# One transformer block on one core: steps without engine loops, another order of VectorE's step, a projection in four passes

## What is computed

```python
h = ln(x)
Q, K, V = h @ wq.T, h @ wk.T, h @ wv.T              # 64 wide each
energy  = einsum('bnd,bne->bde', K, V)              # one 64x64 matrix a batch
x = x + ((Q @ energy) * sqrt(3 / 64)) @ wo.T
h = square(relu(ln(x) @ W_fc.T))                    # 1024 wide
y = h @ W_proj.T
# five steps of a leaky integrate-and-fire neuron driven by y; mean of its spikes
x = x + spikes(y) / 5
```

## Time and profile before

| what | value |
|---|---|
| median of three runs | 505.34 us |
| the profiled execution: its own time | 501.43 us |
| its span (first to last instruction) | 499.5 us |
| mean granted TensorE clock | 0.993 of full |
| TensorE busy | 478.6 us, 96% |
| VectorE busy | 342.4 us, 69% |
| ScalarE busy | 286.4 us, 57% |
| GpSimd busy | 237.3 us, 48% |
| HBM traffic | 17.7 MB read, 8.4 MB written, 52 GB/s |

### The profile page before, as it was taken

How to read it: one execution, slowest core, us unless ns; L and a number is a source line. 1 busy time by engine, 2 the same in 40 slices (tenths; PEclk the granted TensorE clock), 3 DMA queues, 4 the chain that set the end, 5 groups by cost and what they waited for, 6 DMA issues and landing times.

```text
span 499.5 us, 9518 instructions
## 1 busy us (share of the span) xinstructions
PE 478.6 (96%) x3080; PEld 432.7 (87%) x3080; DVE 342.4 (69%) x966; ACT 286.4 (57%) x519; POOL 237.3 (48%) x196
## 2 busy tenths in 40 slices
PE   7899899999999979999999997999999999999995
PEld 6698689899889869898898996898898999999995
DVE  4457658777676776767677855768867674939447
ACT  3427666657566655666566564665746664656540
POOL 1444664473736526374544634545363743535340
PEclk9999999999999999999999998999999999999998
DMA  8413021130403113040312212131110101010102
GB/s 310 99 44 69 17 42 44 54 75 36 93 0 85 43 55 73 0 126 0 85 42 64 63 43 42 43 79 47 55 30 0 42 2 42 1 43 1 44 1 84
DMA packets 60705, 26.46 MB, mean 53 GB/s; under 512 B 55552, under 2 KB 56192, under 8 KB 60416
## 3 DMA queue, kind: packets, MB, share of 16 engines
q1 hardware_dynamic: 60672, 26.09, 19.1%
HBM read 17.69 MB, written 8.39 MB: 52 GB/s over the span
## 4 chain that ended last, share of the span: by engine, by line
PE 79%; DVE 10%; issue 6%; ACT 2%; DMA 1%; POOL 1%; SPq 0%; DVEq 0%; POOLq 0%
PE hid_ps L814 10%; PE hid_ps L815 10%; PE hid_ps L816 10%; PE y_ps L816 10%; PE y_ps L815 10%; PE y_ps L814 10%; PE work_ps L856 3%; PE y_ps L823 2%; DVE stat L592 2%; PE work_ps L922 2%; DVE cnt L701 2%; PE work_ps L923 2%; DVE cnt L720 1%; PE kv_ps L814 1%; PE kv_ps L815 1%
## 5 line engine op out<-in xcount | busy, mean ns | idle before, releaser
L355 POOL TENSOR_TENSOR hid_l<-hid,hid_h 128x512 fp32r<-128x512 f32 x128 | 165.2, 1296 | 204.7 <-ACT hid_h L409 204.5
L398 ACT ACTIVATE relu<-hid_ps 128x512 f32<-128x512 f32 x128 | 76.6, 598 | 112.1 <-PE hid_ps L816 110.6
L815 PE MATMUL y_ps<-wdn_l,hid_h 128*128 128x256 f32 x480 | 136.1, 284 | 0.0
L816 PE MATMUL y_ps<-wdn_h,hid_l 128*128 128x256 f32 x480 | 136.1, 283 | 0.0
L814 PE MATMUL y_ps<-wdn_h,hid_h 128*128 128x256 f32 x480 | 135.7, 283 | 0.0
L814 PE MATMUL hid_ps<-x2T_h,wup_h 128*128 128x512 f32 x256 | 105.5, 412 | 0.5 <-ACT relu L398 0.3
L815 PE MATMUL hid_ps<-x2T_l,wup_h 128*128 128x512 f32 x256 | 100.9, 394 | 0.0
L816 PE MATMUL hid_ps<-x2T_h,wup_l 128*128 128x512 f32 x256 | 100.3, 392 | 0.0
L814 PEld LDWEIGHTS y_ps<-wdn_h,hid_h 128*128 128x128 f32 x480 | 92.0, 192 | 5.1
L815 PEld LDWEIGHTS y_ps<-wdn_l,hid_h 128*128 128x128 f32 x480 | 92.0, 192 | 4.9
L816 PEld LDWEIGHTS y_ps<-wdn_h,hid_l 128*128 128x128 f32 x480 | 91.9, 192 | 0.0
(11 more groups left out here) (125 smaller groups left out, 611.7 us busy)
## 6 DMA issues: line engine op xcount, KB each, us to landing
xs<-x_dram SPq DMA_DIRECT2D x15, 512.0 KB, 3.3
out_dram<-x SPq DMA_DIRECT2D x15, 512.0 KB, 2.7
x_block<-x_dram SPq DMA_DIRECT2D x104, 64.0 KB, 2.5
hid<-w_up_dram SPq DMA_DIRECT2D x1, 1024.0 KB, 8.1
x<-w_down_dram SPq DMA_DIRECT2D x1, 1024.0 KB, 10.2
xs<-x_dram SPq DMA_DIRECT2D x2, 256.0 KB, 2.8
out_dram<-x SPq DMA_DIRECT2D x1, 256.0 KB, 2.0
out_dram<-x SPq DMA_DIRECT2D x2, 128.0 KB, 1.9
```

Of the source, the lines that this page charges most:

```text
L355: nc.gpsimd.tensor_tensor(hid_l[:, i % 2, c, :], hid[:, c % 4, :], hid_h[:, i % 2, c, :].bitcast(f32), ALU.subtract).then_inc(hid_ready, 1)
L398: nc.scalar.activation(relu[:, c % 2, :], hid_ps[c % 2][:, :], ACT.Relu).then_inc(relu_done, 1)
L815: mm(dst, a[0], b[1], start=False, stop=False)
L816: return mm(dst, a[1], b[0], start=False, stop=stop)
```

## The change

- `steps` and SyncE's loop become plain loops of the program that writes the kernel: all 17 steps are written out, with constant semaphore counts.
- VectorE's step begins with the first six of the 12 operations that count the second pair of group i-2 (before: of group i-1, at the end of the step before). Then come `turn_blocks`, `q_low_half`, in odd steps `energy_sum`, the other six counts, in odd steps `eo_low_half`, and then `first_moments`, which stood behind `turn_blocks`. From the residual on the order is as before. GpSimd computes the inverse deviation of group i+3 at c = 4, before at c = 1.
- q takes four passes for six: the two halves of wq lie side by side in `wq_hl`, so one pass of `xT_h` gives high-weight q on partitions 0 to 63 and low-weight q on 64 to 127. Two passes of `xT_l` by the high half of wq alone (64 columns of weights) add to partitions 0 to 63. ScalarE copies only 64 partitions. VectorE takes two dependent operations for the low half: the rest of partitions 0 to 63, written across to 64 to 127 of `kv_scaled`, and then the sum with the lower half of the bank.
- The lead-in has 3, 2, 2 and 12 rounds of idle transposes where it had 8, 4, 2 and 16; ScalarE splits the up weights earlier, VectorE has group 1's `xT_low_half` ahead of its statistics, and `q_low_half(0, 0)` behind K and V of group 1.

```diff
         def steps(eng, step):
-            for i in range(0, FIRST):
-                step(0, i)
-            with eng.Fori(0, LOOPS) as r:
-                for j in range(UNROLL):
-                    step(r, FIRST + j)
-            for i in range(LAST, GROUPS + 1):
+            for i in range(GROUPS + 1):
                 step(0, i)
...
-                    if c == 1 and there(r, i + 3):
+                    if c == (1 if is_first(r, i) else 4) and there(r, i + 3):
                         inverse_deviation(r, 2 if is_first(r, i) else i + 3, 0)
...
-                nc.scalar.activation(qT[:, n % 2, :], q_bank(r, n)[:, :], ACT.Copy).then_inc(q_high, 1)
+                nc.scalar.activation(qT[0:HEAD, n % 2, :], q_bank(r, n)[0:HEAD, :], ACT.Copy).then_inc(q_high, 1)
...
             xT_high_half(0, 1)
+            half_of_columns(w_loaded["up"], wup_raw, wup_h, wup_high, 0)
             kvT_out(0, 0)
+            q_high_half(0, 0)
+            half_of_columns(w_loaded["up"], wup_raw, wup_h, wup_high, 1)
+            kvT_out(0, 1)
             kv_high_half(0, 0)
-            half_of_columns(w_loaded["up"], wup_raw, wup_h, wup_high, 0)
-            q_high_half(0, 0)
-            kvT_out(0, 1)
+            q_high_half(0, 1)
             kv_high_half(0, 1)
-            half_of_columns(w_loaded["up"], wup_raw, wup_h, wup_high, 1)
+            half_of_columns(w_loaded["down"], wdn_raw, wdn_h, wdn_high, 0)
             energy_first_half(0, PER_BATCH - 1)
-            q_high_half(0, 1)
+            half_of_columns(w_loaded["down"], wdn_raw, wdn_h, wdn_high, 1)
             eo_high_half(0, PER_BATCH - 1)
...
                 dve.wait_ge(q_high, upto(r, n + 1))
-                nc.vector.tensor_tensor(qT[HEAD:P, n % 2, :], q_bank(r, n)[HEAD:P, :],
-                                        as_f32(qT[HEAD:P, n % 2, :]), ALU.subtract).then_inc(q_ready, 1)
+                dve.wait_ge(kv_ready, 2 if isinstance(r, int) and n < 3 else upto(r, n + 1))
+                if there(r, n - 1):
+                    dve.wait_ge(q_ready, upto(r, n))
+                nc.vector.tensor_tensor(kv_scaled[HEAD:P, :], q_bank(r, n)[0:HEAD, :],
+                                        as_f32(qT[0:HEAD, n % 2, :]), ALU.subtract).then_inc(q_rest, 1)
+                dve.wait_ge(q_rest, upto(r, n + 1))
+                nc.vector.tensor_tensor(qT[HEAD:P, n % 2, :], q_bank(r, n)[HEAD:P, :], kv_scaled[HEAD:P, :], ALU.add)\
+                    .then_inc(q_ready, 1)
...
+                if there(r, i - 2):
+                    spikes(r, i - 2, 1, range(0, PAIR_OPS // 2))
                 if there(r, i + 3):
                     turn_blocks(r, i + 3)
-                    first_moments(r, i + 3)
                 if there(r, i + 2):
                     q_low_half(r, i + 2)
                 if there(r, i + 2) and closes_batch(i + 2):
                     energy_sum(r, i + 2)
+                if there(r, i - 2):
+                    spikes(r, i - 2, 1, range(PAIR_OPS // 2, PAIR_OPS))
                 if there(r, i + 2) and closes_batch(i + 2):
                     eo_low_half(r, i + 2)
+                if there(r, i + 3):
+                    first_moments(r, i + 3)
...
-                if there(r, i - 1):
-                    spikes(r, i - 1, 1, range(PAIR_OPS))
...
-                for k in range(EC):
-                    last = three(q_bank(r, n)[:, :], (wqq_h[:, k, :], wqq_l[:, k, :]),
-                                 (xT_h[:, n % 2, k, :], xT_l[:, n % 2, k, :]), k == 0, k == EC - 1)
+                both = [wq_hl[:, k, :, :].rearrange("p s d -> p (s d)") for k in range(EC)]
+                mm(q_bank(r, n)[:, :], both[0], xT_h[:, n % 2, 0, :], start=True, stop=False)
+                for k in range(EC):
+                    mm(q_bank(r, n)[0:HEAD, :], wq_hl[:, k, 0, :], xT_l[:, n % 2, k, :], start=False, stop=False)
+                last = mm(q_bank(r, n)[:, :], both[1], xT_h[:, n % 2, 1, :], start=False, stop=True)
...
-            keep_warm(8)
+            keep_warm(3)
...
-            keep_warm(4)
+            keep_warm(2)
...
-            keep_warm(16)
+            keep_warm(12)
```

More of the change, by code:

```diff
@@ L91, in build @@
         wkv_h, wkv_l = (sb(f"wkv_{s}", [P, EC, 2 * HEAD], f32r) for s in "hl")
-        wqq_h, wqq_l = (sb(f"wqq_{s}", [P, EC, 2 * HEAD], f32r) for s in "hl")
+        wq_hl = sb("wq_hl", [P, EC, 2, HEAD], f32r)
         wup_h, wup_l = (sb(f"wup_{s}", [P, EC, HID], f32r) for s in "hl")
@@ L174, in build @@
         averager_ready, mean_done = sem("averager_ready"), sem("mean_done")
-        wkv_centred, wqq_centred = sem("wkv_centred"), sem("wqq_centred")
+        wkv_centred, wq_centred = sem("wkv_centred"), sem("wq_centred")
         wkv_high, wkv_ready = sem("wkv_high"), sem("wkv_ready")
-        wqq_high, wqq_ready = sem("wqq_high"), sem("wqq_ready")
+        wq_high, wq_ready = sem("wq_high"), sem("wq_ready")
         wup_high, wup_ready = sem("wup_high"), sem("wup_ready")
@@ L188, in build @@
         kv_turned, kv_in_scale, kv_high, kv_ready = sem("kv_turned"), sem("kv_in_scale"), sem("kv_high"), sem("kv_ready")
-        q_done, q_high, q_ready = sem("q_done"), sem("q_high"), sem("q_ready")
+        q_done, q_high, q_rest, q_ready = sem("q_done"), sem("q_high"), sem("q_rest"), sem("q_ready")
         energy_done, energy_out, energy_ready = sem("energy_done"), sem("energy_out"), sem("energy_ready")
@@ L301, in _ @@
             load_blocks(0, 3)
[L303 to L309, removed]
+            for i in range(-1, GROUPS):
                 step(0, i)
@@ L519, in _ @@
             high_half_of_weights(wkv_centred, wkv_raw[:, :], wkv_h, wkv_high)
-            high_half_of_weights(wqq_centred, wqq_raw[:, :], wqq_h, wqq_high)
+            act.wait_ge(wq_centred, 1)
+            nc.scalar.activation(wq_hl[:, :, 0, :], wqq_raw.rearrange("p (k s n) -> p k s n", k=EC, s=2)[:, :, 0, :], ACT.Copy).then_inc(wq_high, 1)
             xT_high_half(0, 0)
             xT_high_half(0, 1)
+            half_of_columns(w_loaded["up"], wup_raw, wup_h, wup_high, 0)
             kvT_out(0, 0)
+            q_high_half(0, 0)
+            half_of_columns(w_loaded["up"], wup_raw, wup_h, wup_high, 1)
+            kvT_out(0, 1)
             kv_high_half(0, 0)
-            half_of_columns(w_loaded["up"], wup_raw, wup_h, wup_high, 0)
-            q_high_half(0, 0)
-            kvT_out(0, 1)
+            q_high_half(0, 1)
             kv_high_half(0, 1)
-            half_of_columns(w_loaded["up"], wup_raw, wup_h, wup_high, 1)
+            half_of_columns(w_loaded["down"], wdn_raw, wdn_h, wdn_high, 0)
             energy_first_half(0, PER_BATCH - 1)
-            q_high_half(0, 1)
+            half_of_columns(w_loaded["down"], wdn_raw, wdn_h, wdn_high, 1)
             eo_high_half(0, PER_BATCH - 1)
-            half_of_columns(w_loaded["down"], wdn_raw, wdn_h, wdn_high, 0)
-            half_of_columns(w_loaded["down"], wdn_raw, wdn_h, wdn_high, 1)
             x2T_high_half(0, 0)
@@ L564, in kv_scale @@
                     dve.wait_ge(kv_ready, upto(r, n))
+                if not isinstance(r, int) or n >= 2:
+                    dve.wait_ge(q_ready, 3 if isinstance(r, int) and n == 2 else upto(r, n))
                 by_token = rstd1[:, n % RING, :].unsqueeze(2).broadcast_to([P, TILES, 2 * HEAD])
@@ L780, in step @@
                     kv_low_half(r, i + 3)
-                if there(r, i - 1):
-                    spikes(r, i - 1, 1, range(PAIR_OPS))
             centre_weights(w_loaded["kv"], wkv_raw[:, :], 0, wkv_centred)
-            centre_weights(w_loaded["qq"], wqq_raw[:, :], 1, wqq_centred)
+            centre_weights(w_loaded["qq"], wqq_raw[:, :], 1, wq_centred)
             first_moments(0, 0)
@@ L789, in _ @@
             xT_low_half(0, 0)
-            low_half_of_weights(wqq_high, wqq_raw[:, :], wqq_h, wqq_l, wqq_ready)
+            dve.wait_ge(wq_high, 1)
+            nc.vector.tensor_tensor(wq_hl[:, :, 1, :], wqq_raw.rearrange("p (k s n) -> p k s n", k=EC, s=2)[:, :, 0, :], as_f32(wq_hl[:, :, 0, :]),
+                                    ALU.subtract).then_inc(wq_ready, 1)
+            xT_low_half(0, 1)
             first_moments(0, 1)
-            xT_low_half(0, 1)
             kv_scale(0, 0)
             kv_low_half(0, 0)
-            q_low_half(0, 0)
             kv_scale(0, 1)
             kv_low_half(0, 1)
+            q_low_half(0, 0)
             energy_sum(0, PER_BATCH - 1)
@@ L884, in project_q @@
                     pe.wait_ge(xT_ready, n + 1)
-                    pe.wait_ge(wqq_ready, 1)
+                    pe.wait_ge(wq_ready, 1)
                 else:
                     pe.wait_ge(x2T_ready, upto(r, n - 1))
+                both = [wq_hl[:, k, :, :].rearrange("p s d -> p (s d)") for k in range(EC)]
+                mm(q_bank(r, n)[:, :], both[0], xT_h[:, n % 2, 0, :], start=True, stop=False)
                 for k in range(EC):
-                    last = three(q_bank(r, n)[:, :], (wqq_h[:, k, :], wqq_l[:, k, :]),
```

(3 more changed lines are left out.)

3 lines of the change are left out of this document (removed).

## The result

The changed kernel takes 483.65 us in the median of four runs (483.2 to 484.51); the kernel before, run beside it, 504.99 (504.41 to 507.06). The ratio is 0.957, with a 95% interval of 0.954 to 0.960: faster by 4.3%. Forecast were 485 us and a range of 481 to 493. The profiled execution took 483.47 us, its span is 481.7; before it was 501.43 and 499.5.

What follows compares the result with a forecast made beforehand. TensorE's work and its waits for VectorE were taken as the bound. Terms -3.5, +0.6, -0.9, -5.5 and -9.9 sum to -19.2 us, giving a median of 486.1; 1 us allowed for clock falls made it 485, range 481 to 493.

Steps and rivals of the forecast that it cites:

- Passes of q: TensorE, every group: four passes instead of six save 0.46 us, 5.5 us over 12 groups.
- The waits: TensorE waiting for VectorE's energy in steps that close a batch: removing this saves 9.9 us.
- VectorE's schedule: Times from S, the start of TensorE's step: VectorE's energy is ready 2.1 us early, the residual has 0.7 us cover.
- Instruction loads: Steps written out instead of looped: fetching the extra instructions was priced at nothing.
- Step 0: First step: x2n's turn 0.6 us later through q's second VectorE operation; the next step 0.9 us shorter.
- The lead-in: Before the first step: fewer idle transposes and new orders save 3.5 us, bounds 2.5 to 3.8.
- The walk: Estimated schedule of the new orders before the first step, using durations from profile rows; gave the 3.5 us saving.
- rival 2: TensorE's clock falls before or in the first step, one to three times at 1.5 us: 487 to 490 us; 8%.
- VectorE late (1): In closing steps VectorE's energy or residual overruns its margin, returning 3.9 to 9 us: 489 to 494 us; 16%.
- rival 5: Waits go, but clock and the part before the first step give more than allowed: 479 to 481.5 us; 5%.
- Slow passes (3): TensorE's q passes with 64 weight columns take 0.86 us, not 0.232, giving back 17.6 us: 503 us; 3%.
- instruction loads (4): Written-out steps bring 12 more instruction packets, each stalling TensorE 2.5 us, adding 30 us: 516 us; 3%.

Runs made afterwards that it cites:

- straight_q4: Kernel before with all 17 steps written out and q in four passes, VectorE's step and lead-in in the old order: 497.76 us.
- straight_order: Kernel before with all steps written out and VectorE's step in the new order, q still in six passes, old lead-in: 491.88 us.
- new_pool: Changed kernel with GpSimd waiting for K and V of group 1 before it splits the up weights: 482.02 us.
- changed_again: Changed kernel, unaltered, timed once more in a later set: 483.94 us.
- straight_order_q4: Changed kernel with the old lead-in, except that q_low_half(0, 0) stays behind K and V of group 1: 484.44 us.
- new_warm: Changed kernel with 3 and 4 rounds of idle transposes added in two lead-in gaps where TensorE waits for K and V low halves: 483.04 us.
- new_pool_again: Changed kernel with GpSimd's weight splits behind K and V of group 1, timed again in a later set: 482.14 us.

## Why the prediction was right, and where it was not

**The windows** were right to 0.01 us. Passes of q: 0.46 us a group was forecast, 28.02 - 27.56 was measured. The pass with 64 weight columns costs 0.23, the value taken. The waits: 9.9 us were forecast; together with q's 5.5, 15.4 us between the turns at 84.22 and 455.90. Measured is 371.68 before and 356.25 after (81.71 to 437.96), 15.4.

**VectorE's schedule** was right point by point: energy ready at S+7.9 (7.85), TensorE there at S+10.0 (9.9), residual at S+14.3 with 0.7 of cover (14.3 and 0.59). `straight_q4` and `straight_order` show that this order is what makes the passes pay. The prediction's sum added the two terms without saying that the passes' 5.5 us hold only with the new order: under the old one they cost 1.6.

**Instruction loads** at nothing were right: 23 packets, no idle TensorE. The 2.5 us at a branch back was shown twice, by taking it away and by putting it back (2.10 us).

**Step 0** was forecast 0.6 later and the step behind it 0.9 shorter. From the first matmul of step 0 to the turn that waits for x2n it was 18.76 and is 19.22, +0.5; from there to the next turn 27.84 and 26.80, -1.0.

**The lead-in** was the term that was wrong in size: -3.5 us, with 2.5 to 3.8 as its bounds, and the first matmul of step 0 moved from 37.62 to 35.85, -1.8; x2n's first turn, a sign named for about 31 us, began at 32.53. The part up to K and V was right. Their first matmuls, before and after:

```profile
13.11 0.48 PE L814 MATMUL kv_ps<-xT_h,wkv_h 128*128 128x512 f32 x1
```

```profile
11.11 0.50 PE L815 MATMUL kv_ps<-xT_h,wkv_h 128*128 128x512 f32 x1
```

The walk had 11.05. From there to step 0 it had 23.05 us, and it took 24.74, no less than the 24.51 before. Two things were missing in the walk. The first is contention. VectorE's low halves of K and V, in the changed kernel's lead-in:

```profile
16.71 1.65 DVE L566 TENSOR_TENSOR kv<-kv_scaled,kv 128x512 fp32r<-128x512 f32 x1 [1.73 <-ACT kv L411]
...
19.89 1.25 DVE L566 TENSOR_TENSOR kv<-kv_scaled,kv 128x512 fp32r<-128x512 f32 x1 [0.69 <-ACT kv L411]
...
24.78 0.42 DVE L669 TENSOR_TENSOR eo_l<-e_ps,eo_h 128x256 fp32r<-128x256 f32 x1 [0.29 <-ACT eo_h L433]
```

GpSimd at the same time:

```profile
15.44 5.15 POOL L326 TENSOR_TENSOR wup_l<-hid,wup_h 128x1024 fp32r<-128x1024 f32 x2
20.88 4.80 POOL L326 TENSOR_TENSOR wdn_l<-x,wdn_h 128x1024 fp32r<-128x1024 f32 x2 [0.29 <-ACT wdn_h L376]
```

L566 took 1.65 and 1.25 us, where the walk used 0.69, because the earlier splitting of the up weights put GpSimd's long operations over it: 1.5 us together. `new_pool` shows it by taking GpSimd away: from the first matmul of K and V to step 0 it has 23.19 us, and 23.15 in its second profile, the walk's 23.05 but for 0.1. "SBUF — State Buffer" of the Trainium skill, section "Who interferes with whom", says that a VectorE instruction with two inputs in SBUF contends with a GpSimd instruction that reads SBUF; L566 has two such inputs. The trace agrees, and L650, which reads one input from PSUM, took its 0.68 us beside GpSimd's split of the down weights. The kernel before had a longer time for this operation too, in 12 of its 16, all in its steps. In step 7 GpSimd splits the hidden layer at the same time, from 232.52 to 235.06:

```profile
234.59 1.02 DVE L576 TENSOR_TENSOR kv<-kv_scaled,kv 128x512 fp32r<-128x512 f32 x1 [0.70 <-ACT kv L425]
```

The walk took the 0.69 of the quiet lead-in.

The second is the clock. The event of rival 2, given 8%, happened, though its time, 487 to 490 us, did not. The prediction expected no gap above 2 us in the lead-in and no fall without one like step 9's 3 us; the longest was 2.11, and the clock fell. TensorE in the same stretch:

```profile
21.20 0.66 PE L906 MATMUL e_ps<-kv 128*128 128x128 f32 x4 [2.11 <-DVE kv L566]
21.70 1.44 PE L824 MATMUL y_ps<-ident 128*128 128x128 f32 x8
23.10 1.22 PE L915 MATMUL e_ps<-wo,energy 128*128 128x256 f32 x2
24.12 1.79 PE L824 MATMUL y_ps<-ident 128*128 128x128 f32 x8
```

Behind a gap of 2.11 us, energy times wo takes 1.0 us until the next start and eight transposes 1.5, where they cost 0.43 and 0.9 at full clock. The windows from 20 to 36 us (length, busy by engine, granted clock) of the changed kernel, of `changed_again` and of `straight_order_q4`:

```profile
20.00:36.00 16.00, 14.10 (x103) 12.74 (x104) 11.17 (x29) 3.44 (x6) 6.40 (x4) 0.89 0.11 36
```

```profile
20.00:36.00 16.00, 14.37 (x97) 13.62 (x98) 9.94 (x27) 3.27 (x6) 6.42 (x4) 0.79 0.14 40
```

```profile
20.00:36.00 16.00, 14.76 (x127) 14.18 (x128) 11.03 (x29) 5.14 (x9) 8.09 (x4) 1.00 0.09 34
```

The mean clocks are 0.89, 0.79 and 1.00; worked out from them, TensorE was at 1.2 GHz for about 3.5, 6.7 and 0 us. Of the changed kernel's ten timed executions not one had a mean clock above 0.994 over its span; `straight_order_q4` had 0.998, 0.998, 0.999 and 0.995. So the lead-in edits gained by starting K and V sooner and gave most of it back: 484.44 against 483.65 and 483.94 is what they are worth in the median, 0.5 to 0.8 us, across different sets. `new_warm` shows what preventing the fall alone recovers, 0.6 us from the first matmul of K and V to step 0 (24.13 for 24.74), and `new_pool` that the contention, 1.5 us, is the larger part. A longer stay at half clock costs more: `changed_again` took 25.95 us for the same stretch.

**The median** fell by more than the profiled execution, 21.3 against 18.0 us. The prediction allowed 1 us for falls of the clock behind the long waits; it was 3.4. Part of that is the draw of a few runs: in the last set, where six runs of the changed kernel stand beside eleven of the kernel before, the medians differ by 19.8 us, 1.8 above the profiles. The timed executions of the kernel before show the clock's part:

| kernel before, last set | span, us | mean clock |
|---|---|---|
| slowest | 504.4 | 0.980 |
| next | 503.8 | 0.983 |
| a middle one | 501.7 | 0.986 |
| the two shortest | 499.0, 499.1 | 0.993 |

One run does not fit, 500.3 us at 0.996. The profiled execution, at 0.993, was among the shortest. The kernel written out, whose longest wait in a step is 0.41 us, spreads over 2.5 us in four runs, the changed one over 1.8 in six and `new_pool_again` over 0.6, where the kernel before spreads over 5.2 in eleven. Where exactly the clock fell in those timed executions no trace shows. So that the forecast of 485 came out only 1.35 too high is in part luck. The profiled execution fell by 1.2 us less than forecast, above all because the lead-in gave 1.7 too little; the allowance for the clock was 2.4 too small, and the kernel before took 0.35 less than the 505.34 from which the forecast started. The errors have opposite signs. The mechanism that carries the forecast, 15.4 us between the turns, needed no luck.

**The rivals.** VectorE late (1) did not happen, and the time of rival 5, 479 to 481.5, was not reached. Slow passes (3) and instruction loads (4) are refuted by the rows above.

## What to carry to other kernels

Cutting passes from the busiest engine pays only where it does not then wait for another one: from step 0 on the same edit cost 1.6 us or brought 5.4, by the order of the other engine's step. Compute for each engine when it delivers and when the result is fetched, counted from the start of the step, and keep the difference positive in every kind of step. When work is moved earlier, look at what will run beside it, since durations taken from a quiet stretch need not hold in a full one: VectorE's 0.69 us became 1.65 beside GpSimd. And compare executions by their granted clock before trusting one profile against a median.

## What the runs showed of the hardware that was not expected

- A float32r pass with 64 weight columns over 512 moving columns costs 0.23 us, no less than one with 128 columns.
- A branch back on VectorE costs it 2.1 to 2.5 us, and TensorE no idle time of its own in the trace, although both loop over the same four steps.
- The same two-input VectorE operation took 0.69 us alone, 1.02 in step 7 beside a GpSimd operation of the 128x512 kind, and 1.65 and 1.25 beside those of the 128x1024 kind.
- The clock fell behind gaps of 1.54 and 2.11 us in the changed lead-in and behind 0.57 and 1.55 in `new_pool`. In the old lead-in it did not behind gaps of 1.05 and 1.78 us (`straight_order_q4`), nor behind 0.59 and 1.77 in the kernel before, but did behind 0.60 and 1.78 in `straight_order`. Which executions it strikes stays open.
